# Order of the first TensorE and ScalarE steps in a one-core graph attention kernel: W1's turn first, its products ahead of the first transposes

## The reference

```python
h = jnp.maximum(_layernorm(x, axis=-1), 0.0)
# the layer:
h = inp @ W1 + b1
e = leaky_relu((h @ a1)[:, None] + (h @ a2)[None, :] + b2, 0.2)
attention = softmax(where(adj > 0, e, -1e12), axis=1)
h_prime = attention @ h
return x + elu(h_prime)
```

## Time and profile before

| | |
|---|---|
| median of 3 runs | 423.12 us (422.97 to 427.16) |
| the profiled execution, its own time | 423.61 us |
| its span in the trace | 421.8 us |
| PE busy | 416.8 us, 99% of the span |
| DVE busy | 373.9 us, 89% |
| ACT busy | 308.7 us, 73% |

### The profile page before, as it was taken

The page is one execution under the profiler, slowest core; times in us unless marked ns, Lnnn a source line. Parts: engine busy times, 40 slices in busy tenths (PEclk is TensorE's granted clock), DMA queues, the critical chain, the costliest instruction groups (busy, mean ns, idle before and its releaser), DMA issues.

```text
span 421.8 us, 8476 instructions
## 1 busy us (share of the span) xinstructions
PE 416.8 (99%) x3347; PEld 411.0 (97%) x3347; DVE 373.9 (89%) x404; ACT 308.7 (73%) x306; POOL 30.4 (7%) x44
## 2 busy tenths in 40 slices
PE   9999999999999999999999999999999999999996
PEld 8888899999999999999999999999999999999996
DVE  4897999999998499999995799999992999999945
ACT  4789898999983769957564888768574789586622
POOL 1021100000000400000000400000001200000243
PEclk9999999999999999999999999999999999999999
DMA  8950068555557346648388066647477166576302
GB/s 273 392 209 0 2 215 336 200 200 199 199 200 263 137 170 231 207 147 295 114 309 292 32 211 238 247 144 263 138 266 284 68 232 207 193 246 237 115 4 97
DMA packets 22585, 82.40 MB, mean 195 GB/s; under 512 B 1531, under 2 KB 14113, under 8 KB 14242
## 3 DMA queue, kind: packets, MB, share of 16 engines
q1 hardware_dynamic: 22276, 81.81, 54.9%
q10 hardware_dynamic: 286, 0.27, 0.2%
HBM read 77.86 MB, written 4.21 MB: 195 GB/s over the span
## 4 chain that ended last, share of the span: by engine, by line
PE 97%; DVE 2%; ACT 0%; issue 0%; POOL 0%; DVEq 0%; ACTq 0%; POOLq 0%
PE ps L773 53%; PE ps L775 27%; PE ps L653 5%; PE ps L795 2%; PE ps L796 2%; PE ps L797 2%; PE ps L596 2%; PE ps L641 2%; DVE adj_s L881 1%; DVE h_raw L866 0%; DVE y L1088 0%; PE ps L749 0%; PE ps L730 0%; PE ps L622 0%; PE ps L672 0%
## 5 line engine op out<-in xcount | busy, mean ns | idle before, releaser
L775 PE MATMUL ps<-hp_lo,w_hi 128*128 (+1 forms) x936 | 226.8, 282 | 0.0
L773 PE MATMUL ps<-hp_hi,w_hi 128*128 (+1 forms) x936 | 226.7, 282 | 0.0
L881 DVE SCALAR_TENSOR_TENSOR adj_s<-R,p,adj_s 128x1024 f32<-128x1024 f32 x128 | 165.1, 1330 | 24.2 <-ACT adj_s L451 24.0
L773 PEld LDWEIGHTS ps<-hp_hi,w_hi 128*128 128x128 f32 x936 | 176.8, 189 | 0.0
L775 PEld LDWEIGHTS ps<-hp_lo,w_hi 128*128 128x128 f32 x936 | 176.7, 189 | 0.0
L459 ACT ACTIVATE w_hi<-adj_s 128x2048 fp32r<-128x2048 f32 x64 | 122.3, 1911 | 40.0 <-DVE adj_s L881 39.7
L891 DVE SCALAR_TENSOR_TENSOR w_lo<-adj_s,w_hi 128x2048 fp32r<-128x2048 f32 x64 | 146.0, 2282 | 0.0
L451 ACT ACTIVATE adj_s<-adj_s 128x2048 f32<-128x2048 int32 x64 | 122.2, 1909 | 22.9 <-DMA adj_s<-adj_t 22.5
L773 PE MATMUL ps<-hp_hi,w_lo 128*128 (+1 forms) x944 | 123.1, 283 | 0.0
L773 PEld LDWEIGHTS ps<-hp_hi,w_lo 128*128 128x128 f32 x944 | 117.3, 189 | 0.0
L358 POOL TENSOR_TENSOR y<-y,h_sum 128x2064 f32<-128x2064 f32 x3 | 12.8, 4260 | 271.0 <-ACT y L534 271.0
(11 more groups left out here) (110 smaller groups left out, 193.7 us busy)
## 6 DMA issues: line engine op xcount, KB each, us to landing
adj_s<-adj_t SPq DMA_DIRECT2D x64, 1024.0 KB, 4.9
x_s<-x SPq DMA_DIRECT2D x7, 512.0 KB, 9.0
o_s<-x SPq DMA_DIRECT2D x3, 1024.0 KB, 7.7
out<-o_s SPq DMA_DIRECT2D x6, 512.0 KB, 6.8
R<-r_rows SPq DMA_DIRECT2D x1, 1536.0 KB, 6.4
adj_s<-x SPq DMA_DIRECT2D x1, 1024.0 KB, 5.6
out<-adj_s SPq DMA_DIRECT2D x8, 128.0 KB, 1.7
x_s<-x SPq DMA_DIRECT2D x2, 256.0 KB, 3.9
```

Source lines behind the costliest of these rows:

```text
L773: last = pe.matmul(acc, block_w, hh, start=fresh, stop=False)
L775: pe.matmul(acc, block_w, hl, start=False, stop=False)
L881: last = dve.scalar_tensor_tensor(sgn, R[:, ds(ic * CW, CW)], p[:, ds(source(r, c) + s, 1)], sgn, ALU.max, ALU.mult)
```

## The change

W1's turn comes first on PE, ahead of `turn_vectors` and `spread_b1`. `weigh` moves from behind `transposes(0)` to ahead of `weigh_b1`. ACT copies the turned W1 first, takes the first root ahead of `repeat_b1`, normalises ahead of `keep_b1`, and does `keep_wv` ahead of `keep_ba` and `relu_T(0)`. The counts of matmuls with ones go from 11, 2, 5, 2 to 9, 1, 3, 5. The arithmetic stays the same.

```diff
-WARM = (11, 2, 5, 2)
+WARM = (9, 1, 3, 5)
@@ ScalarE @@
             act.wait_ge(pool_c, 1)
+            keep_WT()
             keep_acol()
-            repeat_b1()
             act.wait_ge(eps_ready, 1)
             root(0)
+            repeat_b1()
+            normalise(0)
             keep_b1()
-            normalise(0)
-            keep_WT()
+            keep_wv()
             keep_ba()
             relu_T(0)
-            keep_wv()
             root(1)
@@ TensorE @@
             keep_warm(WARM[0])
             pe.wait_ge(pool_c, 3)
+            turn_W1()
             turn_vectors()
             spread_b1()
-            turn_W1()
             keep_warm(WARM[1])
+            weigh()
             weigh_b1()
             keep_warm(WARM[2])
             transposes(0)
-            weigh()
             keep_warm(WARM[3])
             pe.wait_ge(w1x_ready, 1)
             project(0, 0)
```

## The result

The changed kernel takes 426.50 us (median of 21 runs, 423.65 to 426.85) against 423.15 us (21 runs, 422.65 to 427.16): ratio 1.0056, 95% interval 1.0041 to 1.0071. This ratio is that of the means, 425.89 to 423.52 us; the medians, which jump between levels, lie further apart (1.0079). The ratios of the experiments aren't quotients of their medians either. The kernel is slower by 0.6%, beyond my range of 422.4 to 425.0, where I had forecast a change of 0.14 us. The single times say more than the median. Of the 21 runs of before, 19 lie at 422.65 to 423.85 and two at 427.09 and 427.16. Of the changed kernel one lies at 423.65; nine lie at 424.9 to 425.4 with a mean granted clock of 0.994 or 0.995, seven at 426.5 to 426.8 with 0.991 or 0.992, and four at 426.6 to 426.9 with 0.998.

What follows compares the result with a forecast made beforehand. PE, full from 13.6 to 40.5 and in the main loop, was taken to hand on any shift in the handovers before 13.61. Their net +0.14 us on the 423.12 median gave 423.3 us, range 422.4 to 425.0.

Steps and rivals of the forecast that it cites:

- Step 1: PE's start: two ones matmuls fewer, W1's four transposes in their place from 5.06, taking 0.85 us; cost 0.
- step 2: ACT copies turned W1 first; acol copy at 6.61, first root at 6.80, first normalise ending at 8.61 against 8.81.
- step 3: b1rep ends at 7.40 against 7.09, weigh starts at 7.58; a new PE wait of 0.6 us ahead of it.
- Steps 4 and 5: transposes(0) start at 9.92, 0.28 us later; projection at 12.00 and second group's transposes at 13.75, each +0.14.
- The sum: +0.14 us at the second group's transposes, 13.61 before, handed on to give 423.3 us; chance 0.55.
- The rival with the late clock: First rise at the start missed: 424.9 us if it comes behind the products, 426.3 if only with the projection; chance 0.14.
- PE has worked for over 5 us by then: Argument against a late clock rise around 6.3: PE already busy over 5 us, transposes under a fifth of it.
- PE is full behind 13.6: PE is busy throughout from 13.6 to 40.5 and in the main loop, so any shift is handed on.
- The spread of before: Runs of one kernel lie from 422.97 to 427.16 us, taken as some tenths on either side of a median.
- D: Theory from experiments: wide work (128 columns or more) missing from a stretch, through idle time or small products, loses the clock.

Runs made afterwards that it cites:

- front alone: Kernel before with only W1's turn moved ahead of turn_vectors on PE, two ones matmuls fewer ahead of it and two more behind spread_b1: 423.29 us, ratio 1.0001.
- the gap of the kernel before: Kernel before without its two middle groups of ones (7 matmuls), so PE waits 0.81 us ahead of transposes(0): 425.89 us, ratio 1.0065.
- the third experiment: Changed kernel with weigh back behind transposes(0), keep_wv behind relu_T(0), four ones matmuls moved ahead of the transposes, b1rep wait kept: 426.18 us, ratio 1.0071.
- weigh at 3: Changed kernel with weigh waiting for acol_kept at 3 instead of 4, so not for b1rep: 424.88 us, ratio 1.0023.
- the shortened wait: Changed kernel with repeat_b1 ahead of root(0) on ScalarE again, PE's wait ahead of weigh 0.28 us: 425.32 us, ratio 1.0040.

## Why the prediction was wrong

Wrong was a sum without a term for the clock, and with it the choice among the cases; the handovers came close, in part by luck. Point by point:

- *Step 1* held in its cost, not in its times: W1's transposes started at 4.87 (5.06 forecast) without a wait, but took 0.56 us instead of 0.85, as the clock was up at 4.4 in this execution and not behind 6.1, so that turn_vectors came at 5.43 instead of 5.97. The front alone gave a ratio of 1.0001.
- *Steps 2 and 3* held in their numbers, and partly by luck: root at 6.72 (6.80 forecast), b1rep's end at 7.32 (7.40), weigh at 7.37 (7.58). ACT's copies were half a microsecond ahead of the forecast and the root waited 0.32 us for DVE's agg, a wait that step 2 did not have. PE's idle time was 0.77 us (0.6 forecast) by the trace's ends; from where the next record could have started, as I counted it, it was 1.03 us (6.12 + 0.22 to 7.37).
- *Steps 4 and 5* held only where the clock does: with the wait filled, the three starts were 10.00, 12.04 and 13.87 against 9.92, 12.00 and 13.75 forecast. That weigh started at 7.59 there, as forecast (7.58), is chance: four more ones set it and not b1rep. The held runs of that variant have a median of 423.82 against 423.35 of before beside them, +0.5 us instead of +0.14. The one held run of the changed kernel, 423.65, lies within the spread of before, so for the change itself that term is neither confirmed nor refuted. In the changed kernel as profiled the starts were 11.61, 15.07 and 16.82.
- *The sum* is the step that failed, in one term. I entered the wait of step 3 as time for which PE only stands behind b1rep, 0.6 us inside a sum of handovers, and took the ones of WARM for filling that can be counted as time. What the wait and the two groups of small products do to the clock had no term. It costs 3.17 us when the clock stays low for 6.8 us, as profiled, and some 2 us in the runs at 425; sixteen of 21 runs have such a fall by their mean clock.
- *The rival with the late clock* had the right kind and size of price, 424.9 to 426.3, but the wrong place and chance (0.14), and my range took in only the first of its two prices. I put its cause at the front, with W1's transposes, in part on the word of the Trainium skill (TensorE: Matmul & The Clock Gate, Part 4), for which I had no row; the front is innocent of the fall by two experiments, the front alone and the 22 transposes. The clock fell after it had risen, 0.4 us into weigh. "PE has worked for over 5 us by then" was no argument, since what follows decides. A late rise, which the rival did name, is likely in four of the 21 runs (426.6 to 426.9, 0.998); the kernel before has 14 such runs in 134 over all sets, so that the change needn't be its cause.
- *"PE is full behind 13.6"* held, and is why the loss is handed on whole: +3.21 us at the second transposes, +3.21 at the main loop, +3.17 in time.
- *The spread of before.* I read 427.16 among the three runs as noise. Most likely it was a late first rise, and the sign that this stretch can lose 4 us by the clock; the two-level pace in the earlier trace rows said where.

What is shown: idle time next to one group of small products (the idle time stands behind the group in the gap of the kernel before, ahead of it in the third experiment), two groups of small products with no idle time (weigh at 3), and the two together (the change) each lose the clock in nearly all runs. Wide ones in the wait take away over half of the loss (a mean of 1.1 us above before, where the change has 2.4), and wide ones between the products, or weigh behind the transposes, the rest; small ones in the same wait take nothing away. D fits all this in direction, but it missed in the share of runs four times (the shortened wait, weigh at 3, fewer ones in the kernel before, ones between the products), so it is no rule. Not run: idle time with no small products near it. Open: why standing apart matters beyond the sum, why single runs of one kernel hold or fall, and what decides on the late first rise. That comes in 14 of 134 runs of the kernel before and in up to four of twelve of the variants, and in all nine that begin with small products; as executions of the same instructions differ in it, the order can't be all of it.

## What to carry to other kernels

In this preamble matmuls on ones weren't idle time to be spent: before an order is changed around such fillers, each stretch in which PE would wait or do products of a few columns must be laid out with what surrounds it, and small products are best kept apart with wide work between them, even where every handover gets earlier. Read PE's pace from start to start, as well as the granted clock, and take a few runs that lie some us above the rest for a second level until it is shown what they are.

## What was not expected of the hardware

- A two-column float32 product occupies PE as long as a 128-column one (0.10 against 0.11 us per record) and doesn't bring up the clock: 22 of them at the start gave 427.38 us, 22 transposes 423.89.
- A wait of only 0.28 us ahead of two groups of such products came with a lost or late clock in all of eleven runs, and no wait at all with a fall in ten of ten.
- With the same PE instructions up to W1's turn, the first rise came at different times, ahead of 5.8 us, behind 6.1 and at 13.9: W1's turn started at 5.81, 6.74 and 7.23.
- At its first level after the start the trace reads a granted clock of 1.00 at half the pace, for 13.9 us in one run.
